# A recurrent layer with a routed spline on one core: earlier splitting of the input weights, two waits of the late products placed elsewhere, and the routing hits turned in fp16

## The reference

```python
def cell(h, x):                                   # a GRU over 1024 positions, 4 batches, D = 1024
    gi = x @ W_ih + b_ih                          # [D, 3D]
    gh = h @ W_hh + b_hh
    i_r, i_z, i_n = jnp.split(gi, 3, axis=-1)
    h_r, h_z, h_n = jnp.split(gh, 3, axis=-1)
    r = jax.nn.sigmoid(i_r + h_r)
    z = jax.nn.sigmoid(i_z + h_z)
    n = jnp.tanh(i_n + r * h_n)
    return (1.0 - z) * n + z * h
...
xf = layernorm(hs) * gamma + beta                 # every token of the GRU's output
best_cluster = argmax(sign(xf) @ cluster_sigs.T)  # 8 clusters of 8 tiles
tile_idx = argmax(where(in_cluster, sign(xf) @ tile_sigs.T, -inf))
x_slice = xf[:, 16 dimensions of the chosen tile] # 64 tiles of 16 dimensions
u = clip((x_slice - tile_min) / (tile_max - tile_min + 1e-8), 0, 1 - 1e-6)
out = x + hs + scatter((base[cell] + slope[cell] * rest) * output_scale)
```

## Time and profile before

| what | value |
|---|---|
| median of 3 runs | 2510.69 us (2509.69 to 2511.22) |
| the profiled execution's own time | 2510.37 us |
| its span | 2508.6 us |
| PE busy | 2354.8 us, 94% of the span |
| DVE busy | 1301.2 us, 52% |
| ACT busy | 661.4 us, 26% |
| POOL busy | 190.5 us, 8% |
| mean granted clock of PE | 0.965 of full speed |

### The profile page before, as it was taken

The page is one execution under the profiler, slowest core; times in us unless marked ns, Lnnn a source line. Parts: engine busy times, 40 slices in busy tenths (PEclk is TensorE's granted clock), DMA queues, the critical chain, the costliest instruction groups (busy, mean ns, idle before and its releaser), DMA issues. The chain is left out here.

```text
span 2508.6 us, 83678 instructions
## 1 busy us (share of the span) xinstructions
PE 2354.8 (94%) x35300; PEld 1294.4 (52%) x35300; DVE 1301.2 (52%) x2682; ACT 661.4 (26%) x1333; POOL 190.5 (8%) x376
## 2 busy tenths in 40 slices
PE   7999999999999989999999999999999999977734
PEld 3444444444444444555666666666666666544411
DVE  4322121212123357676666655666666666888865
ACT  2200000000001223333333333333333333355510
POOL 0000000000000000000000000111111111122217
PEclk9999999999999999999999999999999999999955
DMA  6594131313132455443444444444444444477712
GB/s 213 166 345 163 51 126 51 126 52 129 51 143 101 151 156 153 138 150 116 136 135 135 135 127 111 118 117 117 117 116 117 115 116 119 128 228 233 219 43 4
DMA packets 179894, 330.33 MB, mean 132 GB/s; under 512 B 27856, under 2 KB 89728, under 8 KB 178752
## 3 DMA queue, kind: packets, MB, share of 16 engines
q1 hardware_dynamic: 145360, 267.53, 33.7%
q10 hardware_dynamic: 24192, 44.05, 4.7%
q0 software_dynamic: 10240, 17.31, 4.7%
HBM read 222.13 MB, written 156.77 MB: 151 GB/s over the span
## 5 line engine op out<-in xcount | busy, mean ns | idle before, releaser
L573 PE MATMUL rz_bank<-w_hi,hi 128*32 128x512 f16 x6912 | 422.7, 387 | 52.9 <-DVE hi L869 36.7
L308 DVE SCALAR_TENSOR_TENSOR out_stage<-acc,bias_row 128x512 f32<-128x512 f32 x168 | 116.2, 691 | 629.0 <-PE acc L364 629.0
L362 PE MATMUL acc<-w_hi,x_even 128*128 128x512 f16 x768 | 293.3, 382 | 17.8 <-DVE x_even L300 11.3
L573 PEld LDWEIGHTS rz_bank<-w_hi,hi 128*32 128x32 f16 x6912 | 177.9, 98 | 231.6 <-DVE hi L869 44.8
L363 PE MATMUL acc<-w_hi,x_even 128*128 128x512 f16 x768 | 293.1, 382 | 0.0
L364 PE MATMUL acc<-w_lo,x_even 128*128 128x512 f16 x768 | 292.9, 381 | 0.0
L696 ACT ACTIVATE rz<-sums 128x512 f32<-128x512 f32 x176 | 111.1, 631 | 541.2 <-DVE sums L834 540.9
L834 DVE SCALAR_TENSOR_TENSOR sums<-rz_bank,stage 128x512 f32<-128x512 f32 x176 | 121.5, 690 | 244.9 <-PE rz_bank L573 244.8
L573 PE MATMUL rz_bank<-w_lo,hi 128*32 128x512 f16 x4096 | 243.4, 379 | 0.0
L573 PE MATMUL rz_bank<-w_hi,lo 128*32 128x512 f16 x4096 | 243.4, 379 | 0.0
L573 PE MATMUL n_bank<-w_hi,hi 128*32 128x256 f16 x6912 | 234.8, 279 | 0.0
(11 more groups left out here) (191 smaller groups left out, 2665.3 us busy)
## 6 DMA issues: line engine op xcount, KB each, us to landing
stage<-gi_scratch SPq DMA_DIRECT2D x704, 96.0 KB
gi_scratch<-out_stage ACTq DMA_DIRECT2D x168, 256.0 KB, 2.0
stage<-sums_scratch SPq DMA_DIRECT2D x40, 512.0 KB
stage<-in_xT SPq DMA_DIRECT2D x32, 512.0 KB, 6.4
y<-in_x_rows SPq DMA_DIRECT2D x32, 512.0 KB, 4.4
hs_scratch<-h SPq DMA_DIRECT2D x128, 128.0 KB
x_keep<-hs_scratch SPq DMA_DIRECT2D x32, 512.0 KB, 3.9
y<-hs_scratch POOLq DMA_DIRECT2D x32, 512.0 KB
```

The lines of the kernel that those rows point to most:

```text
L308: nc.vector.scalar_tensor_tensor(out=out_stage[:, tb], in0=acc[e % BANKS][:], scalar=UNSCALE, in1=bias_row[:].rearrange("p q f -> p (q f)" ...
L362: nc.tensor.matmul(acc[e % BANKS][:], hi, wh, start=k == 0, stop=False)
L573: last = nc.tensor.matmul(bank[q * COLS:(q + 1) * COLS, 0:b - a], state[:, s, j], w[:, j, q * QW + a:q * QW + b], start=first and j == 0, ...
```

## The change

The diff has four parts. First, in block 0 of the input product the pieces 4 to 7 are split directly behind the first four, and in the loop over accumulators the piece that is split is e + 8 in place of e + 4; the addition of the two biases on DVE comes behind piece 7. Second, in pe_late the carriers behind the waits go, but for one at the first product of a column block, so that the waits stand at the products themselves. Third, PE's wait for all four late banks moves from ahead of the warm phase to the start of the main pass. Fourth, hit is written in fp16, and PE turns it by a plain fp16 product with ident_sum (a diagonal of 16384) in place of an fp32 transpose with ident; ACT's copy scales by 1/16384.

```diff
+AHEAD = 2 * XPARTS
@@ input_product, scalar
             for m in range(XPARTS):
                 split_w_hi(act, m, m)
                 split_x_hi(act, 0, 0, m * KX)
+            for m in range(XPARTS, AHEAD):
+                split_w_hi(act, m, m)
             for e in range(ACCS):
-                if e + XPARTS < PIECES:
-                    split_w_hi(act, e + XPARTS, e + XPARTS)
+                if e + AHEAD < PIECES:
+                    split_w_hi(act, e + AHEAD, e + AHEAD)
@@ input_product, vector
             for m in range(XPARTS):
                 split_w_lo(dve, m, m)
                 split_x_lo(dve, 0, 0, m * KX)
+            for m in range(XPARTS, AHEAD):
+                split_w_lo(dve, m, m)
             dve.wait_ge(bias_loaded, 5 * 16)
...
             for e in range(ACCS):
-                if e + XPARTS < PIECES:
-                    split_w_lo(dve, e + XPARTS, e + XPARTS)
+                if e + AHEAD < PIECES:
+                    split_w_lo(dve, e + AHEAD, e + AHEAD)
@@ recurrence
-    scores, tkeys, keys, hit, hit_ids = (out_room[:, at + i * NT:at + (i + 1) * NT] for i in range(2, 7))
+    scores, tkeys, keys, hit_ids = (out_room[:, at + i * NT:at + (i + 1) * NT] for i in range(2, 6))
+    hit = out_room[:, at + 6 * NT:at + 6 * NT + NT // 2].bitcast(F16)
@@ pe_late
             pe.wait_ge(late_loaded[k % RING], cb * (KB // RING * 16) + (k // RING * 16 + 16))
-            pe.sem_inc(wait_carrier, 1)
             wh, wl = late_ring[:, k % RING, 0], late_ring[:, k % RING, 1]
             for tb in range(TB):
                 if k == 0:
+                    if tb == 0:
+                        pe.sem_inc(wait_carrier, 1)
                     pe.wait_ge(late_free[tb], cb + 1)
-                    pe.sem_inc(wait_carrier, 1)
@@ pe_turn
-            nc.tensor.transpose(hit_bank[0:NT, 0:P], hit[:], t["ident"][:]).then_inc(hit_turned, 1)
+            nc.tensor.matmul(hit_bank[0:NT, 0:P], hit, t["ident_sum"][:], start=True, stop=True).then_inc(hit_turned, 1)
@@ tensor
             with pe.Fori(0, CBLOCKS) as cb:
                 heads(cb)
-            for tb in range(TB):
-                pe.wait_ge(late_free[tb], CBLOCKS + 1)
             with pe.Fori(WARM_HEADS // 2, WARM // 2) as it:
...
             def one_pass(p, first):
                 seeds = p + 2
+                if first:
+
+                    for tb in range(TB):
+                        pe.wait_ge(late_free[tb], CBLOCKS + 1)
@@ act_hit
-            nc.scalar.activation(hits_t[:, one(tile)].rearrange("t o p -> t (o p)"), hit_bank[0:NT, 0:P], ACT.Copy)\
+            nc.scalar.activation(hits_t[:, one(tile)].rearrange("t o p -> t (o p)"), hit_bank[0:NT, 0:P], ACT.Copy,
+                                 scale=SUM_SCALE / (W_SCALE * S_SCALE))\
```

More of the change, by code:

```diff
@@ L920, in dve_route @@
             dve.wait_ge(hit_turned, T)
-            nc.vector.tensor_scalar(hit[:], keys[:], best[:], None, ALU.is_equal).then_inc(hit_ready, 1)
+            nc.vector.tensor_scalar(hit, keys[:], best[:], None, ALU.is_equal).then_inc(hit_ready, 1)
             nc.vector.scalar_tensor_tensor(out=hit_ids[:], in0=keys[:], scalar=best[:], in1=t["tile_ids"][:],
@@ L1119, in pool_keep @@
             nc.gpsimd.tensor_copy(t["row_i"][:, one(tile)], row_f[:])
-            nc.gpsimd.tensor_copy(hits[:, one(tile)].rearrange("p o t -> p (o t)"), hit[:]).then_inc(hit_kept, 1)
+            nc.gpsimd.tensor_copy(hits[:, one(tile)].rearrange("p o t -> p (o t)"), hit).then_inc(hit_kept, 1)
             pool.wait_ge(row_known, T * 2)
```

## The result

| | median us | range | runs | ratio to before |
|---|---|---|---|---|
| before, same chip | 2510.41 | 2509.14 to 2511.22 | 5 | |
| changed kernel | 2498.28 | 2497.01 to 2499.93 | 5 | 0.995 [0.9939, 0.9961] |

The changed kernel is 12.1 us faster; 13.0 were forecast. Its profiled execution took 2499.93 us with a span of 2498.1 us, 10.4 us less than the one profiled before: it is the slowest of the five, so the profile shows less gain than the median.

What follows compares the result with a forecast made beforehand. PE, busy 94% of the span, was taken to bound the kernel except in the difference steps. Terms 4.8 + 2.8 + 0 + 3.8 + 1.6 = 13.0 us off gave 2497.7 us as the median, range 2492 to 2501.5.

Steps and rivals of the forecast that it cites:

- The gap, 4.8 us: Block 0: splitting pieces ahead lets PE go on at 36.1 us in place of 40.92, 4.8 us less.
- the shortest landing: Block 0: if loads land in the shortest time, 3.8 us, the gap term is 5.5 us.
- The clock of block 0, 2.8 us: Block 0: a remaining wait of 1.7 us should leave PE at 2.4 GHz, saving the half clock's 2.8 us.
- clock falls all the same: Rival, block 0: half clock still follows the shorter wait, so the 2.8 us stay, 2500.5 us; chance 0.10.
- The carriers, 0: Late products: removing the small instructions ahead of the 48 late pieces gains 0.
- the 0.11 us: Ahead of late products: 0.98 us against 0.87, put down to tile shape; rival that it goes, 5.3 us, chance 0.10.
- The late banks, 3.8 us: Start of the warm phase: PE's wait for the last late bank's eviction goes and none replaces it, 3.8 us.
- The slack at lo: First warm step: lo is ready by 1168.1 us, its third part needs it at 1169.5; slack 1.4 us.
- The turn, 1.6 us: Turns in tiles of three-part steps: the fp16 product saves 0.08 us at 20 of 32 turns, 1.6 us.
- The rival that it is no cheaper: Rival: turning hit by a product is no cheaper than the transpose, 2499.3 us; chance 0.12.
- The slow rival: Difference steps: two more half-clock steps in each of ten tiles cost 34 us, 2531.7 us; chance 0.02.
- The sum, 13.0: Whole kernel: 4.8 + 2.8 + 0 + 3.8 + 1.6 = 13.0 us off the profiled 2510.37 us.

Runs made afterwards that it cites:

- e7_biases: The changed kernel with the loads of pieces 4 and 5 ahead of the biases' loads in SP's queue; 2500.91 us (5 runs).
- e5_fill: The kernel before with 26 useless 512-column products in PE's gap ahead of piece 7's low part; 2508.89 us against 2510.92, ratio 0.9992.
- e2_banks: The kernel before with only PE's wait for the late banks moved to the main pass's start; 2505.72 us, ratio 0.9982.
- e9_turn32: The kernel before with hit's turn as a plain fp32 product in place of an fp32 transpose; 2515.21 us in one execution.
- e1_ahead: The kernel before with only the pieces split eight ahead in block 0; 2505.89 us (10 runs), ratio 0.9979.
- e4_turn: The kernel before with only hit in fp16, turned by a product with ident_sum; 2509.26 us (11 runs), ratio 0.9993.
- e3_carriers: The kernel before with only the carriers at the late products changed, waits standing at the products themselves; 2509.69 us (11 runs), ratio 1.0001.
- e8_turn16: The changed kernel with hit's turn as an fp16 transpose in place of a plain fp16 product; 2500.79 us in one execution.
- after_again: The changed kernel as it is, run once more on another occasion; 2498.38 us (5 runs), ratio to the kernel before 0.9948.
- e11_fills2: The changed kernel with useless identity products at the input product's end (130) and the main pass's start (60); 2493.79 us, ratio to the kernel before 0.9931.
- e12_fills3: e11_fills2 with ten more useless 512-column products ahead of the wait for piece 7's low part in block 0; 2494.30 us (5 runs).
- e10_fills: e7_biases with useless identity products at the kernel's start (80), the input product's end (130) and the main pass's start (60); 2498.74 us (10 runs).

## Why the prediction was right, step by step

- **The gap, 4.8 us.** Measured 4.94 in the profile (resumption at 35.98 us, 36.1 worked out). The other profiles with the split order resume between 36.01 and 37.39 us, 3.5 to 4.9 before 40.92; those with the old one between 39.87 and 41.55. The wait itself went from 6.5 to 6.6 us (old order) to 1.5 to 2.8 (new, without a fill ahead of it). Loads 6 and 7 go behind the splits of 4 and 5 as worked out and land 4 to 5 us later. Loading 4 and 5 ahead of the biases bought nothing (e7_biases); whether another place for the biases does is open. (With the shortest landing the term is 5.6 and not 5.5 us; nothing hangs on it.)
- **The clock of block 0, 2.8 us.** The size was right against the one execution that it was read from: 2.80 in the profile and in e5_fill, which takes the half clock alone away. It is no constant of the kernel: from the resumption to block 1 it is 103.61 us at full clock, and in the profiles with the old order 1.35 (e2_banks) to 2.86 us (e9_turn32) more. The reason was weaker than it looked. I inferred from one row, 3.79 us of waiting behind the heads followed by full clock, that a short wait leaves the clock alone. That row was luck: behind the same wait the 32 products took 2.66 us in e1_ahead, 2.35 in e4_turn, 2.47 in e5_fill and 3.60 in e9_turn32, all with half clock in them, and only e3_carriers and the kernel before had none. The row against it, which the rival named, repeats: behind the 3.9 us at the start of the main pass half clock came in all eleven profiles that have this wait. For block 0 the profiles say: full clock behind waits of 1.47, 1.60, 2.15 and 2.57 us, half clock behind 2.35 and 2.84, for 1.7 and 1.4 us. So the forecast of a wait of 1.7 us held where the wait came out near that, with little room, and that part of e1_ahead's shortfall is what an execution on the other side looks like. The rival "clock falls all the same" is thus true in part of the executions.
- **The carriers, 0.** Right: the carriers cost nothing (e3_carriers). That the 0.11 us is the change of tile shape is what is left, not shown.
- **The late banks, 3.8 us.** Right: 3.86 between the late products and the warm step, 4.5 alone (e2_banks). The slack at lo held: the two lo are made from 1162.22 us on, and the third part starts at 1163.99 without a wait. In the profile of the changed kernel 0.75 of it is hidden by the longer half clock at the heads' start.
- **The turn, 1.6 us.** The mechanism was right, the size 0.5 us too large: 0.057 us a turn and not 0.08, 1.1 us for 20. The record is 0.243 us, not the 0.22 I drew from wider products. The rival that it is no cheaper fell.
- **The slow rival.** The difference steps last as long with ten half-clock steps as with hardly any (e7_biases), so its mechanism has no price up to there; no run had the more than one half-clock step a tile that the rival asked for.
- **What the sum left out.** The 1.5 us of "issue" at block 3 stands in all three profiles of the changed kernel's program (1.94, 2.03, and 1.95 in e8_turn16) and in none of the others at more than 0.46. So it is not plain chance, as I had expected of after_again; nor is it PE's earlier arrival: e11_fills2 and e12_fills3 start the last product of block 2 at 388.0 us, as the changed kernel does (388.02), and don't have it. The pair of instruction packets goes with it; what brings the pair in this program stays open, and no run isolates it.

The sum, 13.0, came out at 12.1 (and 12.5 against 2510.90 in after_again). The parts alone give 4.3 + 4.5 + 0.5 + 1.0 = 10.3. Each of these medians is good to about 2 us by its interval, so the difference is not resolved. An interplay would fit, since with the late banks' wait gone no half clock behind it can take back what part 1 gave, but no run of parts 1 and 3 together shows it. That the sum lies within 1 us of the measured gain is in part luck: the delay at block 3 and the oversized turn took away 2 us, and the chance of half clock at several places moves each execution by as much.

## What to carry to other kernels

- Price an idle gap of PE as gap plus clock: here 6.5 us of waiting cost 9.3 in one execution. Fill a gap that can't be removed with useless products if the stage behind it is bound by PE; here two such loops gave 2.7 to 4.5 us, and one ahead of a stage bound by loads 0.5. Run such a kernel often: of e10_fills' ten runs four took over 2508 us, and the cause is open.
- One row of one profiled execution says what can happen, not what does. Where a term rests on the clock behind a short wait, look at several executions before giving it a chance of 0.9.
- The median of two kernels can agree with a sum of stages by chance. Take the difference of the profiled executions apart to its end before giving the gain to the stages that were meant.
- When two engines' in-order queues mix "make the next operand" with "clear the last result", write the makers first as far as the buffers allow: nothing but the order gave 3.5 to 4.9 us.

## What the runs showed of the hardware that I had not expected

- The same wait of 3.79 us is followed by 2.4 GHz in some executions (32 products in 1.91 us) and partly or wholly by 1.2 GHz in others (2.35 to 3.60 us). The runs of one kernel spread by 3 to 6 us (the kernel before by 6.4 in 21 runs); with the idle places filled by 1.5 and 1.9 us in five runs each (e11_fills2, e12_fills3), but e10_fills, which has the same two fills, by 22 us in ten.
- A product of fp32 with 128 columns is two records and holds the queue for 0.36 us, a transpose of fp32 one and 0.23 us, either way of fp16 0.17 to 0.18 us.
- Half clock cost nothing in the difference steps, where PE waits for the vector chain (37 us of waits): 162 us of busy PE and 147 us fill the same 234 us.
- A wait for "issue" of 1.9 to 2.0 us at a loop's edge came in just the three profiles in which two packets of the instruction queue, 1.8 to 2.1 us each, ran at the same time some 4 us ahead of PE's restart.
